# A decoder kernel on one core: scores of two chunks together and a second pass on row halves in its first cross attention

## What is computed

```python
xn = _ln(x, lnx_g, lnx_b)
yn = _ln(y, lny_g, lny_b)
q = jnp.einsum('bsc,hcd->bhsd', xn, wq)
k = jnp.einsum('btc,hcd->bhtd', yn, wk)
v = jnp.einsum('btc,hcd->bhtd', yn, wv)
a = jax.nn.softmax(jnp.einsum('bhsd,bhtd->bhst', q, k) * D ** (-0.5), axis=-1)
o = jnp.einsum('bhst,bhtd->bhsd', a, v)
```

## Time and profile before

| | |
|---|---|
| median of 3 runs | 628.16 us (627.39 to 629.56) |
| the profiled execution | 629.66 us |
| its span in the profile | 627.8 us |
| granted PE clock, mean | 0.98 |
| PE busy | 566.9 us, 90% |
| DVE, POOL, ACT busy | 444.7, 380.6, 372.0 us |
| the changed stage | 116 to 306 us of the span |

### The profile page before, as it was taken

One profiled execution on the slowest core, in us unless ns is written; L12 is line 12 of the kernel. 1 busy time (PEld: TensorE's weight loads), 2 busy tenths in 40 slices (PEclk: granted clock), 3 DMA queues, 4 the chain that ended last, 5 costly groups with the idle time before them and its releaser, 6 DMA issues.

```text
span 627.8 us, 18969 instructions
## 1 busy us (share of the span) xinstructions
PE 566.9 (90%) x8256; PEld 416.1 (66%) x8256; DVE 444.7 (71%) x698; ACT 372.0 (59%) x623; POOL 380.6 (61%) x271
## 2 busy tenths in 40 slices
PE   9788898899999999999888979977889889889897
PEld 4566775566767767666777556664667767778765
DVE  3876728697887887786356774776888988986543
ACT  2335674657657667566462417474677777777552
POOL 1572451488989889864630231175999999977500
PEclk9789999999999999999999999997999999999998
DMA  5830015002101101010013000412422432330000
GB/s 169 238 133 2 3 40 180 2 1 42 34 7 41 26 15 40 3 40 3 2 60 123 2 0 3 99 39 64 103 67 45 96 78 52 78 77 4 2 1 15
DMA packets 33838, 31.81 MB, mean 51 GB/s; under 512 B 27124, under 2 KB 27380, under 8 KB 33756
## 3 DMA queue, kind: packets, MB, share of 16 engines
q1 hardware_dynamic: 33756, 30.60, 18.8%
HBM read 13.06 MB, written 0.23 MB: 21 GB/s over the span
## 4 chain that ended last, share of the span: by engine, by line
PE 62%; DVE 18%; ACT 8%; issue 7%; POOL 3%; DMA 1%; DVEq 0%; POOLq 0%; ACTq 0%
PE psum L1143 9%; DVE scratch L1306 6%; PE psum L1067 5%; PE psum L1119 5%; PE psum L1503 4%; PE psum L1112 4%; PE psum L1114 4%; PE psum L1526 4%; DVE scratch L1291 4%; PE psum L217 3%; POOL scratch L1291 2%; ACT scratch L1276 2%; POOL scratch L652 1%; PE psum L1073 1%; PE psum L248 1%
## 5 line engine op out<-in xcount | busy, mean ns | idle before, releaser
L1291 POOL TENSOR_TENSOR scratch<-scratch 125x896 bf16<-125x896 f32 x143 | 242.7, 1715 | 80.4 <-ACT scratch L1276 79.9
L1306 DVE TENSOR_REDUCE scratch<-psum 128x1 f32<-128x500 f32 x336 | 210.3, 672 | 23.1 <-PE psum L1067 9.6
L1276 ACT ACTIVATE scratch<-psum 125x896 f32<-125x896 f32 x192 | 173.6, 917 | 82.8 <-PE psum L1143 51.1
L1112 PE MATMUL psum<-tok_high,scratch 125*128 125x65 bf16 x1344 | 107.0, 194 | 3.3 <-issue 2.7
L1114 PE MATMUL psum<-tok,scratch 125*128 125x64 bf16 x1344 | 106.4, 194 | 0.0
L1112 PEld LDWEIGHTS psum<-tok_high,scratch 125*128 125x128 bf16 x1344 | 94.8, 98 | 13.9 <-ACT scratch L1276 6.0
L1114 PEld LDWEIGHTS psum<-tok,scratch 125*128 125x128 bf16 x1344 | 88.6, 98 | 17.1 <-issue 0.5
L1143 PE MATMUL psum<-scratch 65*128 65x448 bf16 (+1 forms) x384 | 87.3, 352 | 0.0
L1291 DVE TENSOR_TENSOR scratch<-scratch 125x896 bf16<-125x896 f32 x49 | 67.5, 1383 | 22.8 <-ACT scratch L1276 21.1
L1119 PE MATMUL psum<-tok_high,scratch 125*128 125x65 bf16 x1344 | 72.7, 194 | 4.8 <-POOL scratch L1291 3.1
L1503 PE MATMUL psum<-scratch 128*128 128x500 bf16 x168 | 64.2, 382 | 10.8 <-DVE scratch L1306 6.5
(11 more groups left out here) (340 smaller groups left out, 870.5 us busy)
## 6 DMA issues: line engine op xcount, KB each, us to landing
nrm<-scratch SPq DMA_DIRECT2D x64, 96.0 KB, 2.2
nrm<-w_third SPq DMA_DIRECT2D x32, 96.0 KB, 2.2
raw<-ctx_dram SPq DMA_DIRECT2D x4, 672.0 KB
w_third<-fifth_dram SPq DMA_DIRECT2D x3, 595.0 KB, 6.0
w_third<-third_dram SPq DMA_DIRECT2D x2, 844.0 KB, 8.9
w_third<-third_dram SPq DMA_DIRECT2D x2, 843.5 KB, 6.8
w_fourth<-fourth_dram SPq DMA_DIRECT2D x3, 542.5 KB, 5.8
scratch<-scratch SPq DMA_DIRECT2D x8, 192.0 KB, 2.6
```

What stands on the lines that cost most here:

```text
L1112: nc.tensor.matmul(psum[:, sums, 65 * r:65 * r + 65], rows, t1[:, c, :], start=(c == 0 and r == 0), stop=False, skip_group_check=True)
L1276: nc.scalar.activation(CR["p"][0:CP, n % RING, :].rearrange("p (f n) -> p f n", f=2), psum[0:CP, S:S + 2, 0:HALF], ACT.Exp).then_inc(self. ...
L1291: ops.tensor_tensor(CR["pl"][0:CP, n % RING, :], CR["p"][0:CP, n % RING, :], p_high(n % RING), ALU.subtract).then_inc(done, 1)
L1306: nc.vector.tensor_reduce(mxp[:, r, t:t + 1], bank(B, TB), X_AXIS, ALU.max).then_inc(self.aux_freed, 1)
```

## The change

1. `scores_pe` issues two chunks' scores together, at even chunks: both first passes (the second one waits for the exponentials of the chunk before, as before), then both second passes. At odd chunks it does nothing.
2. The second pass of one half of the columns runs over rows 0 to 63, of the other half over rows 64 to 127. `yb` holds the high tokens twice (two DMAs of 63 rows instead of one of 64), `qb` the low queries of half k in rows 64 k on. For 64 rows to do, the folded weights of feature 0 are subtracted from those of all features (the sum of a normalised token's features is zero, so scores stay), which makes feature 0's query zero, and its row (0 and 64) takes the ones and the shift. `fold_keys_pool` does this once on POOL, ahead of the stage, and `y_ones_set` fills four rows instead of two.
3. The A units cover 448 columns each (4 matmuls each, 8 instead of 7), and ACT copies them to rows 0 and 64.
4. `placement`: M0 to M20 stand in chunks 3 to 9 instead of 4 to 10, N in chunk 3 between the `pv` halves, O first in chunk 6 instead of last in chunk 5. In chunk 3, M0 comes ahead of both `pv` halves.

```diff
-                for c in range(4, 11):
-                    at[c] += [[u] for u in FRONT[3 * c - 10:3 * c - 7]]
+                for c in range(3, 10):
+                    at[c] += [[u] for u in FRONT[3 * c - 7:3 * c - 4]]
...
-                at[3] += [[], [("N", 0)]]
-                at[5] += [[("O", 0)]]
+                at[3] += [[] for _ in range(1 - len(at[3]))]
+                at[3].insert(1, [("N", 0)])
+                at[6].insert(0, [("O", 0)])
...
+        def fold_keys_pool(pool):
+            keys = par("a2_wk").rearrange("p (h d) -> p h d", d=65)
+            nc.gpsimd.tensor_copy(keys[:, :, 64:65], keys[:, :, 0:1]).then_inc(key_scaled, 1)
+            pool.wait_ge(key_scaled, 2)
+            nc.gpsimd.tensor_tensor(keys[:, :, 0:64], keys[:, :, 0:64], keys[:, :, 64:65].to_broadcast([128, HEADS, CD]),
+                                    ALU.subtract).then_inc(key_scaled, 1)
...
+                if n % 2:
+                    return
+                for m in (n, n + 1):
+                    if m >= 2:
+                        pe.wait_ge(self.probs, m - 1)
+                    for f in range(2):
+                        nc.tensor.matmul(bank(2 + 2 * (m % 2) + f, HALF), CR["ya", i][:, chunk(m)],
+                                         CR["qa", i][:, HALF * f:HALF * f + HALF], start=True, stop=False,
+                                         skip_group_check=True)
...
+                for m in (n, n + 1):
+                    for f in range(2):
+                        rows = slice(64 * f, 64 * f + 64)
+                        mm = nc.tensor.matmul(bank(2 + 2 * (m % 2) + f, HALF), CR["yb", i][rows, chunk(m)],
+                                              CR["qb", i][rows, HALF * f:HALF * f + HALF], start=False, stop=True,
+                                              skip_group_check=True)
...
-                sp.dma_start(CR["yb", b % 2][0:64, :], CR["ya", b % 2][64:128, :]).then_inc(self.yb_in, 16)
+                for k in range(2):
+                    sp.dma_start(CR["yb", b % 2][64 * k + 1:64 * k + 64, :], CR["ya", b % 2][65:128, :]
+                                 ).then_inc(self.yb_in, 16)
```

More of the change, by code:

```diff
@@ L1071, in pe_unit @@
                         pe.wait_ge(self.max_set, b + 1)
[L1072 to L1075, removed]
+                    for r in range(3 * k, 3 * k + 4):
+                        lo, hi = max(128 * r, HALF * k), min(128 * r + 128, HALF * k + HALF)
+                        mm = nc.tensor.matmul(psum[:, B, lo - HALF * k:hi - HALF * k],
+                                              nmx[:, r:r + 1].to_broadcast([128, 128]),
+                                              ident16[:, lo - 128 * r:hi - 128 * r], start=True, stop=True)
                 elif kind == "N":
@@ L1133, in scores_pe @@
             def scores_pe(self, pe, n):
[L1135 to L1141, removed]
-                    for f in range(2):
-                        mm = nc.tensor.matmul(bank(S + f, HALF), lhs[0:rows, 128 * c:128 * c + 128],
-                                              rhs[0:rows, HALF * f:HALF * f + HALF],
-                                              start=(rows == 128), stop=(rows != 128), skip_group_check=True)
-                return mm
+                if n % 2:
+                    return
+                b, i = n // CHUNKS, n // CHUNKS % 2
+                chunk = lambda m: slice(128 * (m % CHUNKS), 128 * (m % CHUNKS) + 128)
+                if n == 0:
+                    self.wait_freed(pe, self.index("A", 1, 0))
+                for m in (n, n + 1):
+                    if m >= 2:
+                        pe.wait_ge(self.probs, m - 1)
+                    for f in range(2):
+                        nc.tensor.matmul(bank(2 + 2 * (m % 2) + f, HALF), CR["ya", i][:, chunk(m)],
+                                         CR["qa", i][:, HALF * f:HALF * f + HALF], start=True, stop=False,
+                                         skip_group_check=True)
+                if n % CHUNKS == 0:
+                    self.wait_freed(pe, self.index("A", 1, b))
+                    pe.wait_ge(self.yb_in, 32 * (b + 1))
+                    pe.wait_ge(self.front_low, 2)
+                for m in (n, n + 1):
[4 more added lines that the diff above has]
+                                              skip_group_check=True)
+                        if f:
+                            mm.then_inc(self.scores, 1)
             def run_pe(self, pe, start, projection=None):
@@ L1165, in run_pe @@
                         sums_of_earlier()
[L1166 to L1171 removed]
+                    self.scores_pe(pe, n)
                     if c or not b:
@@ L1221, in copy_act @@
                 if kind == "A":
-                    tile, row = self.shift_row(i)
+                    if b and self is cross1:
+                        self.wait_freed(act, self.index("Q", 1, b))
+                    lo, hi = HALF * k, HALF * k + HALF
+                    tile, row = self.shift_row(i, k)
                     nc.scalar.activation(tile[row:row + 1, lo:hi], psum[row:row + 1, B, 0:hi - lo], ACT.Copy
@@ L1389, in run_pool, with tokens_pool @@
                         self.low_part(pool, nc.gpsimd, n, self.low_pool)
[L1390 to L1395 removed]
+                    if b < BATCH - 2:
+                        self.tokens_pool(pool, b, c)
+            def tokens_pool(self, pool, b, c):
+                if c in (1, CHUNKS - 1):
+                    if b:
+                        pool.wait_ge(self.pv_done, CHUNKS * b)
+                    if b == 2:
+                        pool.wait_ge(cx_rstd, 2)
+                    self.split_tokens(pool, b + 2, int(c > 1))
             def turn_tokens(self, sp, b):
@@ L1423, in plan @@
             def plan(self):
-                return [("K", k) for k in range(3)] + FRONT[2:], (1, 2), (1, 2)
+                return [("K", k) for k in range(3)] + FRONT[2:], (1, 2)
             def place(self, b):
```

72 lines of the change are left out of this document (43 added, 29 removed).

## The result

The changed kernel takes **641.97 us** (median of 4 runs, 639.37 to 643.34), the kernel before, run beside it, 628.86 us (627.39 to 632.31). The ratio is 1.0185, its 95% interval 1.0143 to 1.0227: slower by 9 to 14 us. The forecast was 634.0, in a range of 628.5 to 639.5. The direction was right, the size less than half of it. The profiled execution took 641.96 us (span 639.9), against 629.66 (span 627.8).

The account below looks back on a forecast made before the run. PE was taken as the bound before, then a loop through the tokens and M0. Six periods +4.8, first sequence +2.1, end -1.5 and pair waits 0.4 made +5.8 on the median of 628.16: 634.0 us, range 628.5 to 639.5.

Parts of the forecast that it names:

- Tokens to M0: From chunk 10's exponentials through split and turn to M0's start: 9.57 us plus 0.1 for a stretched split.
- The rival that POOL and DVE lock each other: Token split 0.4 instead of 0.1 us longer, +1.8 over six periods: 635.8; with whole drains 640; chance 0.15.
- Pair of scores: Two chunks' second passes on PE take 0.57 instead of 0.76 us, two tile changes included; 48 pairs save 9.1.
- Changes of tile: Rival: going to 64-row tiles and back costs 0 instead of 0.093 us, giving back 5.7: 628.3; chance 0.13.
- the last rival: The second pass's row halves do not run side by side: a pair costs 0.38 us more, about 650; chance 0.03.
- M0 waits, the rest queues: In chunk 3 PE waits some 1.3 us a sequence for tokens; N, `pv` of chunk 1 and next scores queue behind.
- M0 to chunk 10, the sum of 15.64: PE's work from M0 to the next chunk 10's exponentials grows from 13.42 to 15.64 us; loop 25.3, +4.8 over six periods.
- The clock, taken as 1.00 throughout: PE's granted clock in the changed stage, read as 1.00 (2.4 GHz); the sum had no term for a fall.
- The turn, taken as 3.70 each time: The tokens' transpose, issued at 192.06 with the copy behind it at 195.76, inside the 9.57 us before M0.
- First sequence: Sequence 0, where tokens are already there: a later Q1 subtraction and the added PE terms cost +2.1 us.
- The 0.4 for waits of pairs: Allowance of 0.4 us, bounds 0 and 2, for pairs' waits on POOL and DVE that could not be laid out.
- PE stays the bound: Rival: tokens land before PE reaches M0, so all 9.1 us of saved PE work comes off: 619.1; chance 0.07.

Follow-up runs that it names:

- halves_serial: Changed kernel with both halves of the second pass on rows 0 to 63 instead of on different row halves; 649.99 us.
- place_only: Kernel before with only the new places of M, N and O, scores still one chunk at a time; 642.39 us.
- tokens_early: Changed kernel with the second half of the token split on POOL in chunk 3 instead of 11; 638.82 us.
- tokens_q1_early: Changed kernel with the token split's second half in chunk 3, and Q1's copies and subtraction ahead of chunk 2's exponentials and low part; 641.09 us.
- warm_m0: Changed kernel with 12 fill-in matmuls of 256 columns on PE ahead of M0's wait for the tokens; 638.58 us.

## Why the prediction was right or wrong

**Tokens to M0: right.** 9.68 for 9.67. From the split's start to the turn's issue it was 3.27 (223.39 to 226.66, where the forecast had 3.13 and 0.1), though differently: L1401 went up to 1.68 beside DVE's low part, and the cast came down to 0.50. The rival that POOL and DVE lock each other for 0.3 longer did not come.

**Pair of scores: right.** 0.49 for the second pass, 0.09 to 0.1 for each change of tile. Changes of tile were not free, nor a whole drain of 0.16. That the Trainium skill, TensorEngine Tiling (Array Packing), Key Properties, has a change of tiling mode drain the engine agrees in that it is paid for, at the 0.09 of the rows. halves_serial rules out the last rival.

**M0 waits, the rest queues: right.** The wait was 1.40 (forecast 1.3), and place_only shows that the places alone make the slowdown, 1.07 of the 1.19 of a period. The pairs in these places neither save nor cost much: the PE time that they free goes into the wait for the tokens.

**M0 to chunk 10, the sum of 15.64: too small by 0.41.** The forecast took away the wait behind N for ACT (0.3) and put nothing for DVE there. But M0 to M2 now fall at a time when DVE is still busy with chunk 2 and Q1, and M2 waits 0.31. That wait is gone in tokens_early, where DVE's low part of chunk 1 is not stretched to 2.49, and is 1.4 in tokens_q1_early, where DVE's low part of chunk 2 stands behind Q1. Behind O the M took some 0.1 more than the 0.3 of the forecast. A period was 25.72 for 25.3: over six, 7.1 us instead of 4.8, an error of **2.3**. The step that failed is the term for M behind N: the wait for ACT was taken away and none for DVE put in its place.

**The clock, taken as 1.00 throughout: wrong, 2.4.** This step failed by as much as DVE's pace did: the sum costed the waits as idle time alone. It had no term for what PE's idling does to the matmuls behind it. The changed kernel's trace shows two stretches at half clock; warm_m0, without them, puts the first at 1.2, and the second is 1.2 by difference (2.0 of the fifth period less the 0.76 of its turn). Why the clock fell behind that wait of 2.15 and not behind the 2.21 of place_only is open.

**The turn, taken as 3.70 each time: wrong, 0.8 to 0.9.** The earlier trace rows hold one turn of the six in the stage. The longer ones were in the trace of before too, hidden (below); the change took that cover away, and the forecast did not price it. It cost the fifth period 0.8 and the sixth, whose turn took 4.18, 0.2: there M2's wait for DVE, 0.31, fell away against the 0.48.

**First sequence: +3.9 for +2.1.** 1.2 of the difference is the clock, already counted. The rest is 0.6; part of it is M waiting for DVE's maxima (0.8 us in this sequence, 0.4 before), and what is left is not taken apart. **End: right**, -1.4 for -1.5. **The 0.4 for waits of pairs** were not seen apart.

2.3, 2.4, 0.9 and 0.6, less the 0.4 and rounding, make the 5.8 us by which the stage of the profiled run missed. The fills and the fold were hidden as said: POOL was through with them at 90.37 and idled 3.62 before its next work. The start of the stage was 2.7 later, of which 2.1 stood already at 36 us, where POOL's 16th operation came at 38.40 instead of 36.27, before any changed instruction; the program behind the stage was 2.2 shorter. I have no cause for that but the granted clock of the run, and leave it there.

The range failed because its upper end, 639.5, was built of one more lock and full drains; nothing in it covered a wait that is longer in some sequences and slows what follows. And "PE stays the bound" was treated as the main way to faster: that the place of another unit (O) decides how much of the pairs' 9 us comes through was not among the rivals.

## What to carry to other kernels

When work is moved ahead of what it waits for, price the whole chain of limits behind the first one (here tokens, then the query copy, then VectorE), and allow a TensorE wait more than its length: the matmuls behind it may run at half clock, as in two places here, and every late transfer now counts. Here the saving on the bounding engine came through, by half, only where its units stood where the next engine could keep up; look for a unit without a consumer at hand (here O) and put it into the remaining idle stretch. Compare stage lengths in the traces when whole times scatter by more than the effect.

## What the runs showed of the hardware

**A DMA transpose with a code load inside it takes longer.** The DMA view of the usual turn (issued at 226.66) and of the long one (252.38), first its queues, then its landing:

```profile
q1 hardware_dynamic: 1568, 0.39, 52.8%
scratch<-tok SPq DMA_TRANSPOSE x1, 3.7
```

```profile
q1 hardware_dynamic: 1568, 0.39, 72.6%
q8 instruction: 1, 0.02, 1.3%
scratch<-tok SPq DMA_TRANSPOSE x1, 4.4
```

The same 1568 packets, and one load of 16 KB on the instruction queue between them. In all twelve traces, from a turn's issue to the copy behind it in the changed stage: with no load inside, 3.68 to 3.78 us; with one of 16 KB that began 0.3 to 2.9 us behind the issue, 4.06 to 5.17, in each of 16 cases; with one of 16 KB at 3.1 to 3.4 us, anything from 3.68 to 5.42; with one of 8 KB at 3.1 to 3.2 us, 3.77 to 3.88, and at 3.6 to 3.7 us, 3.70 to 3.73. No run removes the loads, so this is a pattern and not a test. The kernel before had one of 5.42 in its last period and hid it: that period is 24.52. Why some late ones cost nothing is open.

**Half clock behind a short wait.** In the changed kernel M0 after a wait of some 1.4 to 1.6 ran at full clock in four sequences and after one of 1.87 in a fifth; after 2.15 it did not. In halves_serial the clock fell to 0.50 behind a wait of 1.81, in place_only it stayed at 1.00 behind 2.21 and 2.08. With fill-in matmuls ahead, a wait of 1.27 left it at 1.00. So the length of the last wait alone does not decide it. This is what PE did in each case, one trace each, and no rule.
